# Half-size expert tiles in a decoder layer's mixture of experts, and its routing rearranged

## The reference: what is computed

```
h2 = rmsnorm(X, norm2_w)                       # 4096 tokens x 256
probs = softmax(h2 @ router_w)                 # 8 experts
topw, topi = top_k(probs, 2); topw = softmax(topw)
combine = sum(one_hot(topi, 8) * topw[..., None], axis=1)
swiglu(x, g, u, d) = silu(x @ g) * (x @ u) @ d  # 256 -> 512 -> 256
shared = swiglu(h2, sh_gate, sh_up, sh_down)    # every token
out = X + shared + sum over e of combine[:, e] * swiglu(h2, e_gate[e], e_up[e], e_down[e])
```

## Time and profile before

| what | us |
|---|---|
| median of three runs | 1155.63 |
| the profiled execution | 1154.84 |
| its span | 1153.0 |
| head of phase two, first `turn` to the first tile unit | 613.15 to 742.34 |
| the 39 tile units | 742.34 to 1100.43 |
| the three shared units after them, end of TensorE | 1100.43 to 1131.08 |
| the tail after TensorE | 1131.08 to 1153.0 |

### The profile page before, as it was taken

One profiled execution on the slowest core, in us unless ns is written; L12 is line 12 of the kernel. 1 busy time (PEld: TensorE's weight loads), 2 busy tenths in 40 slices (PEclk: granted clock), 3 DMA queues, 4 the chain that ended last, 5 costly groups with the idle time before them and its releaser, 6 DMA issues. The chain is left out here.

```text
span 1153.0 us, 32693 instructions
## 1 busy us (share of the span) xinstructions
PE 1076.8 (93%) x13012; PEld 1011.7 (88%) x13012; DVE 805.8 (70%) x1367; ACT 620.1 (54%) x1266; POOL 551.0 (48%) x542
## 2 busy tenths in 40 slices
PE   3789999999999999999966999999999999999992
PEld 2678889989898989898865999999999999999992
DVE  1668778777778777788645644577777777777746
ACT  1244555555555555566544333466666666666635
POOL 4243334344343344434201477346666666666754
PEclk8999999999999999999986999999999999999996
DMA  7585455454654444541215422368878887878548
GB/s 211 101 192 106 94 95 107 114 115 91 131 111 91 120 108 74 103 71 35 93 38 167 165 102 97 125 202 230 239 232 236 231 226 219 224 233 230 139 76 244
DMA packets 294679, 167.73 MB, mean 145 GB/s; under 512 B 220688, under 2 KB 266000, under 8 KB 293648
## 3 DMA queue, kind: packets, MB, share of 16 engines
q1 hardware_dynamic: 278064, 141.05, 45.5%
q0 software_dynamic: 14880, 22.09, 9.4%
q10 hardware_dynamic: 1584, 2.49, 0.6%
HBM read 121.74 MB, written 54.15 MB: 153 GB/s over the span
## 5 line engine op out<-in xcount | busy, mean ns | idle before, releaser
L1580 POOL DMA_INDIRECT total_scratch<-kept_late,slot_meta x78 | 135.4, 1736 | 110.6 <-DMA total_scratch<-kept_late,slot_meta 58.5
L1450 DVE TENSOR_TENSOR prod<-kept_weights,up 128x512 f32<-128x512 f32 x110 | 75.2, 683 | 144.2 <-ACT kept_weights L1290 144.2
L1569 POOL TENSOR_TENSOR act_lo<-prod,act_hi 128x512 fp32r<-128x512 f32 x78 | 120.3, 1686 | 36.5 <-ACT act_hi L1297 36.5
L1297 ACT ACTIVATE act_hi<-prod 128x512 fp32r<-128x512 f32 x110 | 69.5, 632 | 111.1 <-DVE prod L1450 109.7
L1290 ACT ACTIVATE kept_weights<-gate 128x512 f32<-128x512 f32 x110 | 64.8, 589 | 110.6 <-PE up L1221 110.6
L678 ACT ACTIVATE p3t<-psum 128x512 f32<-128x512 f32 x128 | 68.8, 596 | 89.2 <-PE psum L527 89.2
L929 POOL TENSOR_TENSOR ctx_lo<-ctx_t,ctx_hi 128x512 fp32r<-128x512 f32 x16 | 20.6, 1288 | 139.8 <-ACT ctx_hi L588 139.8
L849 DVE TENSOR_REDUCE max<-psum 128x16 f32<-128x2048 f32 x32 | 73.3, 2292 | 18.2 <-PE psum L513 18.2
L368 PE MATMUL psum<-kept_room,x_hi 128*128 128x512 f32 (+1 forms) x256 | 62.4, 367 | 18.3 <-POOL x_lo L925 18.3
L1274 ACT ACTIVATE we_hi<-w_raw 128x1024 fp32r<-128x1024 f32 x78 | 77.7, 1044 | 0.0
L1221 PE MATMUL gate<-tok_hi,we_hi 128*128 128x256 f32 x312 | 67.7, 298 | 1.2 <-DVE we_lo L1434 0.7
(11 more groups left out here) (277 smaller groups left out, 3404.7 us busy)
## 6 DMA issues: line engine op xcount, KB each, us to landing
w_raw<-in_w_gate SPq DMA_DIRECT2D x26, 512.0 KB, 3.6
w_raw<-in_w_up SPq DMA_DIRECT2D x26, 512.0 KB, 4.5
w_raw<-in_w_down SPq DMA_DIRECT2D x26, 512.0 KB, 6.2
slots_scratch<-in_empty SPq DMA_DIRECT2D x39, 258.0 KB, 3.8
kept_weights<-slots_scratch SPq DMA_DIRECT2D x39, 258.0 KB, 6.0
raw_gate<-in_w_gate SPq DMA_DIRECT2D x13, 512.0 KB, 3.6
h_rows<-in_w_up SPq DMA_DIRECT2D x13, 512.0 KB, 4.5
h_rows<-in_w_down SPq DMA_DIRECT2D x13, 512.0 KB, 6.2
```

What stands on the lines that cost most here:

```text
L1297: act.activation(act_hi[:, n % 2, h * FH:(h + 1) * FH, :], prod[:, h, :].rearrange("p (f n) -> p f n", f=FH), ACT.Copy).then_inc(act_hi_do ...
L1450: dve.tensor_tensor(prod[:, h, :], silu[:, h, :], up[h][:, :], ALU.mult).then_inc(prod_done, 1)
L1569: pool.tensor_tensor(act_lo[:, n % 2, h * FH:(h + 1) * FH, :], prod[:, h, :].rearrange("p (f n) -> p f n", f=FH), act_hi[:, n % 2, h * FH: ...
L1580: pool.indirect_dma_start(out=scratch["total"], out_offset=bass.IndirectOffsetOnAxis(ap=slot_meta[:, i % METAS, j, 0:1].bitcast(I32), axis=0),
```

## The change

Three things change together.

**Half tiles.** The 39 tiles of 256 rows become 31 full tiles and 9 half tiles of 128 rows, 40 tiles in all, 56 units. The order is four full tiles, then nine times three full and one half. In a half tile the tokens are the stationary operand (`still rows`) and 256 weight columns move, so that `gate` and `up` take 6 matmuls a half of the channels where a full tile takes 12, of the same 128x256 shape. The products then come out with tokens on the partitions, so TensorE turns them (`turn_products`, four transposes), and hi and lo are made from the turned ones: hi on ScalarE (`half_hi`), lo on VectorE (`half_lo`) and not on GpSimd. `down` takes 12 matmuls. The weights are the same size as a full tile's: three loads, three splits on ScalarE, three on VectorE.

**Routing.** GpSimd makes the lo part of the shared expert's `up` and `down` weights, VectorE only that of `gate`. `count_tiles` moves from unit 1's first half to the end of unit 0 and is longer, and so is `find_slots`, since rows may now lie in full or half tiles. VectorE writes the choice weights into the rows, all first ones at once after `weigh`, the second ones one group a unit from unit 2 on (`second_weights`). GpSimd's sends lose their copies and come in another order.

**Twelve shared units in front.** 12 shared units stand before the tiles and four after them, and four pairs of sequences, where it was two, get their moments inside the last units (`FINISHED`); two are normalised there too (`NORMALIZED`).

```diff
@@ sizes
-BEFORE = 13
-TILES = 2 * B * S // UT + E - 1
+BEFORE = 12
+FULL = 2 * B * S // UT - 1
+HALF = E + 1
+TILES = FULL + HALF
-ROWS = TILES * UT
+ROWS = FULL * UT + HALF * P
-FINISHED = (0, 0, 2)
-NORMALIZED = (0, 0, 0)
+FINISHED = (0, 0, 2, 4)
+NORMALIZED = (0, 0, 0, 2)
...
+        SENDS = [(0, 0), (1, 0), (2, 0)]
+        for g in range(GROUPS):
+            SENDS += [(g, 1), *([(g + 3, 0)] if g + 3 < GROUPS else [])]
...
+        ORDER = [*range(FULL - 3 * HALF), *(x for h in range(HALF) for x in (*range(FULL - 3 * (HALF - h), FULL - 3 * (HALF - h) + 3), FULL + h))]
...
+        def parts_of(n):
+            i = tile_of(n)
+            return 2 if i is None or ORDER[i] < FULL else 1
+        def is_half(n):
+            return parts_of(n) == 1
...
@@ TensorE
                         if h == 0:
-                            pe.wait_ge(w_lo_done, split_count(n, kind))
+                            pe.wait_ge(*lo_done(n, kind))
+                        if is_half(n):
+                            for m, (wp, hp, dk) in enumerate(terms):
+                                at = dk * DFF + h * FH * P
+                                mm = pe.matmul(bank[:, 0:FH * P], hp[:, n % 2, dk, 0:P], wp[:, kind, at:at + FH * P],
+                                               start=(m == 0), stop=(m == 3 * DK - 1))
+                            continue
...
+                def turn_products(n):
+                    pe.wait_ge(prod_done, 2 * n + 2)
+                    for f in range(FT):
+                        mm = pe.transpose(turned[n % 2][:, f * P:(f + 1) * P], prod[:, f // FH, f % FH * P:(f % FH + 1) * P], ident[:, :])
+                    mm.then_inc(act_turned, 1)
...
+                    if is_half(n):
+                        turn_products(n)
                 down_unit(UNITS - 1)
@@ ScalarE
+                def half_hi(n):
+                    act.wait_ge(act_turned, halves_upto(n))
+                    act.wait_ge(down_ready, n - 1)
+                    act.activation(act_hi[:, n % 2, :, 0:P], turned[n % 2][:, :].rearrange("p (f n) -> p f n", f=FT), ACT.Copy)\
+                       .then_inc(act_hi_done, 2)
...
@@ VectorE
+                def second_weights(g):
+                    b = slice(g * GB, (g + 1) * GB)
+                    dve.wait_ge(scattered[g % 3], 16 * GB * (g // 3 + 1))
+                    dve.tensor_copy(rows_of(b)[:, :, D + 1], rows["w2"][:, b]).then_inc(weights_written, 1)
...
+                def half_lo(n):
+                    dve.wait_ge(act_hi_done, 2 * n + 2)
+                    dve.tensor_tensor(act_lo[:, n % 2, :, 0:P], turned[n % 2][:, :].rearrange("p (f n) -> p f n", f=FT),
+                                      act_hi[:, n % 2, :, 0:P].bitcast(F32), ALU.subtract).then_inc(half_lo_done, 1)
...
-                ROUTING = {(0, 0): (choose_second,), (0, 1): (weigh,), (1, 0): (count_tiles, find_slots), (1, 1): (place,)}
+                ROUTING = {(0, 0): (choose_second,), (0, 1): (weigh, count_tiles), (1, 0): (find_slots,), (1, 1): (place,)}
                 largest()
                 token_lo(0)
-                for kind in range(3):
-                    split_lo(0, kind)
+                split_lo(0, 0)
...
+                    elif is_half(n):
+                        half_lo(n)
...
+                    if SECOND_FROM <= n < SECOND_FROM + GROUPS:
+                        second_weights(n - SECOND_FROM)
@@ GpSimd
+                for kind in (1, 2):
+                    pool.wait_ge(w_hi_done, kind + 1)
+                    pool.tensor_tensor(ws_lo[:, kind, :], kept["weights"][:, kind, :], ws_hi[:, kind, :].bitcast(F32),
+                                       ALU.subtract).then_inc(shared_w_lo, 1)
...
                 for k, (g, which) in enumerate(SENDS):
-                    pool.wait_ge(gate_up_ready, 4 + k)
+                    pool.wait_ge(gate_up_ready, 3 + k)
                     if which == 0:
                         pool.wait_ge(h_loaded[g], 16 if g else KEPT)
-                    weights_of_choice(g, which, k)
+                    else:
+                        pool.wait_ge(weights_written, 2 + g + 1)
                     scatter(g, which)
...
                 for n in range(FIRST_TILE, AFTER_TILES):
                     i = tile_of(n)
-                    routed_lo(n, 0)
+                    if not is_half(n):
+                        routed_lo(n, 0)
                     if i >= 2:
                         add_tile(i - 2)
-                    routed_lo(n, 1)
+                    if not is_half(n):
+                        routed_lo(n, 1)
```

203 lines of the change are left out of this document (127 added, 76 removed).

## The result

The changed kernel takes 1164.85 us, the median of seven runs (1162.01 to 1170.2); the kernel before took 1155.63 beside it. The ratio is 1.0088, with a 95% interval of 1.0073 to 1.0102: it is slower, by 9.2 us, or 0.9%. The profiled execution took 1164.68, its span 1162.9.

The account below looks back on a forecast made before the run. It took TensorE's 9.03 us a unit and VectorE's loop of 8.7 to 9.25 as near-equal limits. Head +1.2, tile stage +1.3, end +7.6, tail -2.9 gave +7.2: span 1160.2, time 1163 us, range 1150 to 1171.

Parts of the forecast that it names:

- End and tail: Behind the tiles: one more shared unit, +7.6 us to TensorE's end; fewer moments left behind TensorE, -2.9 us.
- The head: Start of phase two up to the tile units: later slots, a wait and a slower clock start the tile stage +1.2 us.
- The moved unit is paid as a wait: At the first tile's `turn`: TensorE arrives earlier, waits 6.9 us for the slots, then loses 2.0 us to a lower clock.
- GpSimd's blocking: Head: GpSimd's two weight splits stop VectorE's two-input instructions in `choose_first`, +0.9 us, bounds 0 and +2.4.
- the longer routing: Head: the longer `count_tiles` and `find_slots` on VectorE make `slot_index` 1.45 us late.
- the sends: Head: GpSimd's sends lose 16 copies of 0.19 us, -3.1 us to the last scatter.
- The half tile by its own steps: Tile stage: VectorE's splits and second product hold a half tile to 9.1 us, bounds 8.9 and 9.7.
- The step that failed: In a half tile: GpSimd's last `act_lo` began near t = 2.6 and took 1.89 us; `down` waits until 4.5.
- the third rival: Half tiles: a blocked first split of 1.84 us decides each, 1.05 us more a group, 1172 us; chance 0.08.
- TensorE's pace: Tile stage: half tiles run at TensorE's pace, 7.8 us each, 23.8 us less, 1139 us; chance 0.11.
- halfway: Tile stage and head: shorter loops, half tiles of 8.5 us, early wait 2 us shorter, 1153 us; chance 0.17.
- A lower clock in half tiles: Half tiles: TensorE's clock falls in each of nine, 1.7 us each, 1178 us; chance 0.04.

Follow-up runs that it names:

- the experiment with VectorE's splits: The changed kernel with the lo parts of all three shared weights on VectorE again, none on GpSimd; ratio 1.0057 to the kernel before.
- a quarter of the columns: The changed kernel with VectorE's three lo splits in half tiles covering 256 of 1024 columns, the rest left out; stage 356.39 us, ratio 1.0086 to the kernel before.
- the kernel with the product first: The changed kernel with 13 shared units in front and, in half tiles, the second product ahead of the weight splits; ratio 1.0042 to the kernel before.
- the repeat: The changed kernel run once more, unaltered, for a second trace; 1168.15 us, tile stage 367.50.
- the kernel with the new routing alone: The changed kernel's routing, GpSimd splits, choice weights and sends with 39 full tiles, no half tile, 13 shared units in front; ratio 1.0058 to the kernel before.

## Why the prediction came out right

The time, 1163.0 against 1164.85, is right within the forecast's own range, but two of its four terms were off by 2.7 and 5.3 in opposite directions.

- **End and tail, right.** +7.6 against +7.70, -2.9 against -2.99.
- **The head: mechanism right, sizes off.** The moved unit is paid as a wait, 6.33 where 6.9 was forecast and above the bound of 3, with 7.99 from that `turn` to the tiles against 6.25 (1.74 of clock; 2.0 forecast). Two sizes were too dear. `slot_index` came 1.2 later relative to the phase, not 2.35: of it GpSimd's blocking is 0.6 (the experiment with VectorE's splits) where 0.9 was taken, and the longer routing 0.6 where 1.45 was. The product behind `count_tiles` started at 636.20, which is 0.88 behind the earlier trace rows relative to the phase, GpSimd's 0.6 included, where 1.1 was taken for `count_tiles` alone (whose own pieces in the forecast sum to 636.8 and not 637.1). And the sends gained 3.8, not 3.1 (from `slot_index` to the last scatter 83.90, before 87.71). 0.65 more is the start of phase two, which is not the change's. The Trainium skill's rule, "SBUF — State Buffer", section "Who interferes with whom" (the two exclude one another for a whole instruction), is borne out by the rows: two-input instructions stand still for as long as GpSimd's runs, and the reduction between them does not. It was its length that was overestimated, since only two of the two-input instructions were under it; `choose_first` has four of them, not five.
- **The half tile by its own steps, right where GpSimd is early.** In the unit at 877.15 the product starts at t = 2.55 (forecast 2.55), the first split at 4.46 (4.5), the second product ends at 8.27 (8.5) and the next unit starts at 8.74 (9.1). It is VectorE's loop: with a quarter of the columns the unit falls to 7.86. In the eight half tiles that have a tile behind them the second product never came before t = 7.5. The 30 other full tiles sum to 268.4, and the forecast's to 268.9.
- **The step that failed: GpSimd's last `act_lo` ends near t = 4.5 in every half tile** ("began near t = 2.6 and took 1.89"). In five of eight half tiles it ended a microsecond or more later, and the unit took 9.73 or more. That is the third rival's condition, "runs past t = 4.5", which I had given 0.08. I weighed it by the subtractions that GpSimd loses, and not by what stands ahead of them in its queue: scatter-adds, of which each waits until the tile before has landed. That price is +3.4 in the half tiles (0.7 of it the clock's) and +3.9 in one unit of 12.94 (where +1 had been allowed for such). In the kernel with the product first, a second table of sums takes away that wait alone, and with it every late `act_lo`, every long unit, and 20 us.
- **TensorE's pace** (first rival, 1139) and **halfway** (1153) fell for the same reason: where VectorE's part was cut or moved, the landings took much of the gain or all of it. (The argument for halfway miscounts too: a half tile takes two subtractions off GpSimd, so a group has two fewer, not four.) Half tiles of 7.8 in every group, as the first rival has them, came only with the product first and the landings out of the way. **A lower clock in half tiles** came, but seldom and cheaply: once in this trace, behind the wait of 2.34, and not behind the four of 1.8; three times in the repeat, in two half tiles and the long unit. At 0.7 a time that is not the rival's 1.7 in each of nine. The forecast's tile stage has no term for it. The Trainium skill, "TensorE: Matmul & The Clock Gate", "HAM oscillation — how this bites in real kernels", has the clock fall in every turn of a loop, behind waits for data longer than these. Here it fell behind shorter ones, and behind waits of one length (1.8) only some of the time, which that section doesn't foresee.

So the size owes something to luck: errors of -2.7 and +5.3 that cancelled in part. The sign doesn't: end and tail alone are +4.7, the head gave back 1.5 of it, and no half tile ran at TensorE's pace.

## What to carry to other kernels

Before you take work off the busiest engine, write down every loop of nearly its length, and of each the queue it shares: here TensorE's 9.03, VectorE's 8.7 to 9.25 and a chain of scatter-adds and landings of about 9, which no busy share shows, since GpSimd is busy 45% of the time. Ask of an instruction on which others wait what stands ahead of it in its queue and what that waits for. And a stage put behind a fixed arrival gives nothing when it is taken from in front of it: the engine waits for the arrival, and the clock with it.

## What the runs showed of the hardware

Two of the chips lose 15 to 35 us in the head of phase two, whatever the kernel: 144.4 and 148.0 with 12 units in front where the others have 128.3 to 128.7, and 157.8 to 163.7 with 13 where they have 129.0 to 129.3. On them TensorE stops from about 658 us on, several times, for 0.4 to 1.7 us between two matmuls, with no releaser. TensorE in the kernel with the new routing alone:

```profile
661.61 0.76 PE L1291 MATMUL down<-ws_hi,act_hi 128*128 128x256 f32 x3 [0.92 <-issue]
662.17 0.41 PE L1291 MATMUL down<-ws_lo,act_hi 128*128 128x256 f32 x1
663.75 0.59 PE L1291 MATMUL down<-ws_lo,act_hi 128*128 128x256 f32 x2 [1.17 <-issue]
665.85 0.37 PE L1291 MATMUL down<-ws_lo,act_hi 128*128 128x256 f32 x1 [1.52 <-issue]
```

It starts where loads and scatters together had the DMA engines 99% busy for 10 us (652 to 662, 381 GB/s), which they are in the kernel before on its chip too without a stop (650 to 660, 1.00 and 392 GB/s), and goes on after that has ended. Between 656 and 676 us TensorE is busy 8.90 of 20 us and the clock is at 0.64, where the kernel before on its chip has 20.00 and 1.00. No run tells what it is; that the queue that fetches instructions is late there is a guess, since in the stretch from 650 to 680 this trace shows none of its packets, four others with such stops one each, and five traces without them two each.

The wait behind which TensorE's clock falls isn't one length. In the tile stages of these runs the granted clock went to 0.50 behind waits of 1.79 (992.64 in the repeat), 1.93, 2.06, 2.34 and 6.84 us, and stayed at 1.00 behind others of 1.79, behind one of 2.25 (a quarter of the columns) and behind one of 2.60. Behind the waits of about 1.04 in the changed kernel's two traces it stayed up. The tile stage of the kernel before has no wait over 0.9 and no fall.
